# Attention's projections: six units of a pair in one visit of every second slot, three PSUM banks in rotation

## The reference

```
q, k, v = x @ W_q[h], x @ W_k[h], x @ W_v[h]        # x: 4 x 1024 x 256, 16 heads of 64
attn = softmax(q @ k^T * 1/(64*64*16)) @ v          # 1024 x 1024 scores for each head
x = layernorm(x + concat(attn) @ W_o)
probs = softmax(x @ gate_W); top 2 of 8 experts, weights normalised
out = 0.5*gelu(x @ shared_W + b) + sum_e combine_e * (gelu(x @ W1[e] + b1[e]) @ W2[e] + b2[e])
x = layernorm(x + out) * gamma + beta
```

## Time and profile before

| | |
|---|---|
| median of three runs | 1801.71 us |
| the profiled execution | 1799.77 us, span 1798.0 us |
| TensorE | busy 1737.0 us, 97% of the span |
| VectorE | busy 1363.6 us, 76% |
| ScalarE | busy 1035.7 us, 58% |
| GpSimd | busy 399.3 us, 22%, nothing of it in the slots |
| attention's slots | from 32.6 us to 1136 us of the span |
| exponentials, line 533 | 512 of 1030 ns |
| additions, line 649 | 384 of 1225 ns |

### The profile page before, as it was taken

How to read it: one execution, slowest core, us unless ns; L and a number is a source line. 1 busy time by engine, 2 the same in 40 slices (tenths; PEclk the granted TensorE clock), 3 DMA queues, 4 the chain that set the end, 5 groups by cost and what they waited for, 6 DMA issues and landing times. The chain is left out here.

```text
span 1798.0 us, 32053 instructions
## 1 busy us (share of the span) xinstructions
PE 1737.0 (97%) x11007; PEld 1201.3 (67%) x11007; DVE 1363.6 (76%) x2196; ACT 1035.7 (58%) x1529; POOL 399.3 (22%) x442
## 2 busy tenths in 40 slices
PE   9999999999999999999999999999779999999977
PEld 7555555555555555555555555799679999999972
DVE  6888888888888888788888889776656665565647
ACT  6555655655565565555556566476445555465537
POOL 1000000000000000000000000016756666677654
PEclk9999999999999999999999999999889999999998
DMA  5011111111111111311121111464223443334335
GB/s 182 31 36 48 36 36 42 36 36 36 48 36 36 42 36 42 118 51 36 36 88 36 42 36 36 149 204 152 96 80 90 90 90 89 48 90 90 88 66 168
DMA packets 80199, 127.12 MB, mean 71 GB/s; under 512 B 12752, under 2 KB 46736, under 8 KB 77776
## 3 DMA queue, kind: packets, MB, share of 16 engines
q1 hardware_dynamic: 61808, 98.27, 16.4%
q0 software_dynamic: 18272, 27.31, 7.7%
HBM read 86.72 MB, written 38.83 MB: 70 GB/s over the span
## 5 line engine op out<-in xcount | busy, mean ns | idle before, releaser
L533 ACT ACTIVATE a_e<-banks 128x1024 f32<-128x1024 f32 x512 | 483.2, 1030 | 192.6 <-PE banks L429 192.6
L649 DVE TENSOR_TENSOR a_esum<-a_esum,a_e 128x1024 f32<-128x1024 f32 x384 | 470.5, 1225 | 141.8 <-ACT a_e L533 108.3
L443 PE MATMUL banks<-a_e,a_v 128*64 128x512 f32 x2048 | 467.5, 598 | 0.0
L443 PEld LDWEIGHTS banks<-a_e,a_v 128*64 128x64 f32 x2048 | 135.5, 136 | 266.3 <-issue 242.6
L64 POOL MEMSET ident<- 128x128 f32 x1 | 0.2, 205 | 1118.8 <-POOLq L167 1118.8
L429 PE MATMUL banks<-a_qh,a_kh 64*128 64x512 f32 x1024 | 218.5, 420 | 2.6 <-DVE a_kl L586 1.6
L429 PE MATMUL banks<-a_qh,a_kl 64*128 64x512 f32 x1024 | 203.5, 390 | 0.0
L429 PE MATMUL banks<-a_ql,a_kh 64*128 64x512 f32 x1024 | 203.3, 390 | 0.0
L1884 ACT ACTIVATE e_g<-banks,e_b1c 128x256 f32<-128x256 f32 x280 | 115.7, 470 | 150.5 <-PE banks L1832 146.0
L429 PEld LDWEIGHTS banks<-a_qh,a_kh 64*128 64x128 f32 x1024 | 96.8, 183 | 110.9 <-issue 75.7
L1845 PE MATMUL banks<-woh,e_hh 128*128 128x256 f32 x560 | 162.3, 290 | 1.4 <-issue 0.2
(11 more groups left out here) (254 smaller groups left out, 3354.3 us busy)
## 6 DMA issues: line engine op xcount, KB each, us to landing
attn_out<-a_ot SPq DMA_DIRECT2D x64, 256.0 KB, 2.0
a_inv<-inv_rows SPq DMA_DIRECT2D x126, 128.0 KB, 2.8
a_w<-w_qkv SPq DMA_DIRECT2D x32, 256.0 KB, 3.1
raw<-attn_out SPq DMA_DIRECT2D x4, 2048.0 KB, 11.5
raw<-w_up SPq DMA_DIRECT2D x8, 1024.0 KB
raw<-w_down SPq DMA_DIRECT2D x8, 1024.0 KB
t_ot<-attn_out SPq DMA_DIRECT2D x3, 2048.0 KB, 9.9
raw<-x_t SPq DMA_DIRECT2D x8, 512.0 KB, 9.4
```

The source lines that it names most:

```text
L443: mm = pe.matmul(o_acc[h * DH:(h + 1) * DH, :], v[quad % 2][:, n, head], e[(slot * ST + n) % NE][:, h * BANK:(h + 1) * BANK], start=n == 0 ...
L533: act.activation(e[t % NE], ring[place(n) % RING], ACT.Exp, scale=SCALE).then_inc(e_ok, 1)
L649: dve.tensor_tensor(acc[:, :], acc[:, :], e[(slot * ST + n) % NE], ALU.add).then_inc(add_ok, 1)
```

## The change

The slot with m = 0 has no units any more. The slot with m = 1 has all of them for pair i+1, in the order Q0, K0, Q1, K1 and then, where there is a next quad, V0, V1 (`units`). Three banks are taken in rotation (`UNIT_BANKS`): the two halves of the ring's place, and `side`. Units 0, 1 and 2 wait as before for their bank's last user; units 3, 4 and 5 wait until unit 0, 1 or 2 of the same slot has left its bank. In a slot without units the ring's ninth place is empty, and score tile 6, which takes the same buffer next, waits for the exponential of tile 1 instead. In the token stage one load by SP waits for one more tile of `otl_ok` than before.

```diff
             i, m = slot // NB, slot % NB
             out = []
+            if m < NB - 1:
+                return out
             if i + 1 < B * PAIRS:
-                out += [(Q, i + 1, m), (K, i + 1, m)]
+                out += [(kind, i + 1, part) for part in range(NB) for kind in (Q, K)]
             if i // 4 + 1 < QUADS:
-                out.append((V, i // 4 + 1, i % 4 * NB + m))
+                out += [(V, i // 4 + 1, i % 4 * NB + part) for part in range(NB)]
             return out
+
+        UNIT_BANKS = 3
+
+        def units_in(slot, bank):
+
+            return [u for k, u in enumerate(units(slot)) if k % UNIT_BANKS == bank]
...
             slot, k = visit[u]
+            k = k % UNIT_BANKS
             return side if k == 2 else ring[HALF % RING][:, k * BANK:(k + 1) * BANK]
...
                 slot, k = visit[u]
-                if k < 2:
+                if k >= UNIT_BANKS:
+                    wait_evacuated(pe, units(slot)[k - UNIT_BANKS])
+                elif k < 2:
                     pe.wait_ge(e_ok, slot * ST + occupant(slot, HALF)[1] + 1)
-                elif slot and len(units(slot - 1)) > 2:
-                    wait_evacuated(pe, units(slot - 1)[2])
+                elif slot >= NB and units_in(slot - NB, 2):
+                    wait_evacuated(pe, units_in(slot - NB, 2)[-1])
...
                 held, tile_held = occupant(slot, place(n))
+                if held >= 0 and tile_held is None and not units(held):
+                    held, tile_held = occupant(held, HALF)
                 if held >= 0 and tile_held is None:
-                    for u in units(held)[0:2]:
+                    for u in units_in(held, 0) + units_in(held, 1):
                         wait_evacuated(pe, u)
...
-                    sp.wait_ge(otl_ok, HALF)
+                    sp.wait_ge(otl_ok, HALF + 1)
```

## The result

Timed on one chip, 22 runs of each: before 1802.38 us (median; 1798.83 to 1807.46), after 1807.62 us (1805.71 to 1812.13). The ratio is 1.003, with a 95% interval of 1.0023 to 1.0036. The change costs 5.2 us (4.1 to 6.5 by the interval); forecast were 6.7, and 1808.4 us. The profiled execution of the kernel after has a span of 1805.5 us.

What follows compares the result with a forecast made beforehand. TensorE was taken to bound the kernel, 17.45 us a slot. Terms +0.4 + 7.0 + 0.9 - 1.6 = +6.7 us on the profiled 1799.77 gave 1806.5; with 1.9 to the median, 1808.4 us, range 1802.5 to 1812.

Steps and rivals of the forecast that it cites:

- opening: Slot 0, where score tiles 4 and 5 wait for ACT's first exponentials: +0.9 us (0.6 to 1.2).
- six pairs with rows: Pairs where DVE's subtraction of the next batch's rows precedes Q0's: K1 waits 1.3 us, 6 x (1.13 + 0.04) = +7.0 us.
- plain pairs: The 21 of pairs 1 to 27 without rows of the next batch: +0.02 us each, +0.4 us (-0.8 to +2.5).
- slot 40: The 15.45 us the inverse denominators take are covered with 0.5 to spare, so TensorE's earlier loss goes: -1.6 us.
- last three pairs with units, without V: Both orders lose the same 12 matmuls: 0 us.
- K1 waits because of DVE's queue: K1 needs Q0's bank, whose subtraction stands behind DVE's queue from addition 4 of slot B: wait 0.17 us.
- The hand-over: From the end of DVE's subtraction to the start of K1's matmul: 0.14 us.
- the latenesses do not add: ACT's late exponential and DVE's lateness do not add; rival that they add, 0.25 us more a pair, 1815 us, chance 0.06.
- The rival that small waits cost nothing: K1's wait and ACT's lateness are taken in; plain pairs keep 0.15 to 0.2 us each: 1804.3 us, chance 0.17.
- Visits: TensorE's visit to the units costs 0.21 us for coming and going; one of two goes in 31 pairs, 6.5 us.
- The rotation hides it all: Rival: two further units cover Q0's copy and subtraction, K1 never waits: -7.0 us, 1794.7 us, chance 0.08.
- The waits cost the clock: Rival: a stretch of half clock after each of six longer waits in slots B: +10 us, 1818 us, chance 0.03.

Runs made afterwards that it cites:

- moving the rows: Kernel after, with DVE's subtraction of the next batch's rows moved from slot A to slot B, behind the units' subtractions: 1791.73 us, ratio 0.9991 to before.
- the units' order: Kernel after, with the six units ordered V0 Q0 K0 V1 Q1 K1: 1795.4 us, ratio 0.9978 to the kernel before.
- The doubled step: DVE's subtraction of the weights in slot A done twice: in the kernel after 1827.14 us, ratio 1.016; in the kernel before 1803.76 us, ratio 1.0023.
- either edit alone: Kernel after with ACT's weights cast ahead of the output copy (1797.44 us), or with DVE's weights subtraction behind slot B's units' subtractions (1795.18 us).
- both: Kernel after with ACT's weights cast ahead of the output copy and DVE's weights subtraction behind slot B's units' subtractions: 1791.39 us, ratio 0.9992 to before.
- The divided slot 0: Kernel after with rows' and weights' subtractions in slot B, ACT's weights cast earlier, and pair 1's units divided over slots 0 and 1: 1782.77 us, ratio 0.9944.
- the first two experiments: Kernel after with the rows' subtraction moved to slot B (1791.73 us), and with ACT's weights cast ahead of the output copy (1797.44 us).
- the next four: Kernel after with weights' subtraction in slot B (1795.18 us), that plus earlier cast (1791.39), those plus rows' subtraction in slot B (1793.79), another units' order (1795.4).

## Why the prediction was right

The time from the two traces, by the first matmul of the values of each slot B, with the terms of the forecast:

| | forecast | measured |
|---|---|---|
| opening, to the second scores of slot 1 | +0.9 | +1.03, of which 0.22 ahead of the first scores |
| six pairs with rows | +7.0 | +6.7 |
| plain pairs | +0.4 | -0.4 (19 x -0.02), and +0.24 in pair 19 |
| slot 40 | -1.6 | -1.66 |
| last three pairs with units, without V | 0 | -0.68 |
| sum | +6.7 | +5.2 |

*K1 waits because of DVE's queue.* Right: laid out were 13.58 + 0.61 + 13.58 = 27.77 us from addition 4 to Q0's subtraction; after has 27.75. That the place and not the length of the subtraction matters is shown by moving the rows (-7.0 us) and by the units' order (-9.4). The doubled step shows it too: 0.72 us a pair in after, nothing in ordinary pairs of before.

*The hand-over.* Mis-sized. The 0.14 us from the subtraction's end to the matmul was read from a wait of the scores at 775.98. At K1 it is 0.06: 652.82 - 652.76 above, and the same in the other five pairs with rows and in all K1 waits of the doubled step. The forecast for the plain pair, 588.31 + 27.75 + 0.68 + 0.14 = 616.88, comes within 0.02 of the start at 616.90, but that is luck. The bank was free at 616.80. TensorE by itself came to K1 at 612.64 + 0.11 + 3 x 1.37 = 616.86, because ACT had made it late.

*Six pairs with rows.* Forecast 1.13 + 0.04 longer than before, measured 1.12 each. The wait at K1 was forecast as 1.3 and is 0.90, or 1.05 by the distance of the two matmuls (1.28 instead of 0.23). Most of the difference is the shorter hand-over, 0.08, and ACT's 0.12, by which TensorE comes later to K1. Since DVE alone sets the length of these pairs, ACT's lateness changes the wait and not the pair.

*Plain pairs.* Mis-sized: "I take +0.02", measured -0.02, 19 times. The wait at K1 of 0.17 and the restart of 0.08 did not take place (the 0.40 of the matmul at 616.90, and 0.24 to the next): K1's weight load waits for DVE, its matmul doesn't. A plain pair loses 0.12 in slot A, to ACT, and 0.04 to 0.09 in the visit (8.47 us, where visits without any wait take 8.38 or 8.43), which is 0.16 to 0.21 against the 0.21 saved. My own lower end of -0.04, no restart, was nearly the case. That the latenesses do not add is shown by either edit alone giving 0 to 0.06 and both giving 0.18. The rival that small waits cost nothing was right about K1 and wrong in the main: it wanted 34.7 in plain pairs, and that came only when both latenesses were taken away.

*Visits.* That one is worth 0.21 us was read from two distances and is shown by the pairs without waits: 34.68 against 34.89. Before, two visits a pair, and then one. What it is the price of, the prediction had wrong: "between products on whole and on half rows of the array". The values ahead of the units also use all 128 rows (128*64 in their row), and the change from values to the scores' half rows stays when the visit goes. The visit adds one more change, from 128*64 to 128*128: its second matmul comes 0.34 later instead of 0.23, and the scores start 0.32 behind its last one instead of 0.23, together 0.20. The Trainium skill (TensorEngine Tiling (Array Packing), Key Properties) says that changing the tiling mode drains TensorE; it gives no price. No run here separates such draining from another cause of the 0.21.

*Slot 40.* Right in size, but closer than forecast. The inverse denominators landed at 770.30, 0.1 us before DVE needed them; 0.5 was forecast. The transfer took 15.8 us from the reciprocal's end, not 15.45. Had it come later than that 0.1, DVE would have waited; the doubled step in before shows what such a wait can cost.

*The opening.* The exponential of tile 2 released tile 4 at 36.72, the values started at 39.96 against 39.8 forecast. Without the 0.22 ahead of the first scores the opening costs 0.81. The divided slot 0 gives 0.87 back.

*The last three pairs.* Forecast 0, since both orders lose the same 12 matmuls. These pairs too have one visit less, 0.21 each, which I had left out. They took 0.25, 0.37 and 0.06 less, 0.68 together; the last has the wait of 0.50 at K1. How the rest comes about is not shown.

*The rotation hides it all.* Not for this order of the queues. The rule of the Trainium skill (Perfetto Trace Analysis, Matmuls) on rotating independent groups through banks came true with the same three banks once the evacuation (the subtraction that frees the bank) stood early enough, ratio 0.9971, or the bank was asked for later, 0.9978.

*The waits cost the clock.* Wrong here: the granted clock was 1.00 over all slots, with six waits of 0.9 to 1.0 us. It stayed so with the doubled step in after, where six waits at K1 were 1.65 to 1.69 us. The swing of the clock that the Trainium skill (TensorE: Matmul & The Clock Gate, A second HAM failure mode: psum-queue depth-cycling) tells of did not come about in these slots.

*Open.* Pair 19 is 0.24 longer in after and in the first two experiments, and not in the next four. DVE's queue to Q0's subtraction was 723.26 - 695.25 = 28.01 us there instead of 27.75: addition 1 of slot A started 0.43 us behind the reciprocal's start instead of 0.27. Where DVE or TensorE's order had room, this reached no matmul. What held the addition is not shown. The scatter of the stage behind the slots was not looked into further.

## What to carry to other kernels

A bank in rotation is free when its evacuation's turn comes in its engine's queue: lay the queue out from that engine's last idle moment, and put occasional work (weights, the next batch's rows) behind the evacuation, or take first the units whose banks need only one engine. When work is gathered into one place, the pause that it gave another engine elsewhere goes too; whatever that pause took in silently is then paid in full, 1.13 us six times here at a busy share of 83%. Two small latenesses that meet at the same instruction hide each other: each edit alone measures as nothing (0 and 0.06 us a pair), both together 0.18. And a step taken out of a chain of steps that wait for each other can give back less than its length, if it stood in a pause of the chain: here 0.42 of 0.60.

## What the hardware showed unexpectedly

A wait of TensorE of 2.52 us was followed by 3.4 us of granted clock 0.50; one of 1.34 us at the same place was not, nor were the waits of 0.9 to 1.0 us in after and the six of 1.65 to 1.69 with the doubled step: the clock stayed 1.00. So in this one case a long wait cost more than itself: 1.18 us more of waiting cost 2.65.

The same release takes a different time at different places: 0.06 us from the end of DVE's subtraction to the matmul of a unit, 0.15 to one of the scores (775.84 to 775.98, and four waits of the doubled step in before). Why they differ is not shown.

Additions of 128x1024 that wait for each other start 1.33 us apart on DVE; an instruction that waits for none of them starts 1.14 behind one. So such an instruction between two of them cost 0.42 instead of its 0.60.

A restart of TensorE after a wait, and the first unit or score after a product of another shape, shows in the timeline as a matmul of 0.50 us instead of 0.39 or 0.40 and a next one 0.31 to 0.34 later instead of 0.23. It marks waits too short to be listed, as at 636.46 us.
